# An adaLN transformer block on one core: q and k in two float32r parts and 64-row tiles instead of three bf16 parts and the full array

## The reference, cut to what matters

```python
h = layernorm(x) * (1 + ca) + sa
x = x + ga * attention(h)        # 16 heads of width 16, causal
h = layernorm(x) * (1 + cb) + sb
x = x + gb * ffn(h)              # layernorm, attention with 32 heads of width 8,
                                 # no mask, then 2 experts per batch with gelu
# in both attentions, for each head:
scores = q @ k.T / sqrt(d)       # 512 x 512, q and k are fp32
attn   = softmax(scores)
out    = attn @ v
```

## Time and profile before

| | |
|---|---|
| median of 3 runs | 1867.98 us (1866.65 to 1868.94) |
| profiled execution, first to last instruction | 1866.4 us |
| PE matmul busy | 1646.4 us, 88% |
| PE weight load busy | 717.9 us, 38% |
| VectorE busy | 1197.6 us, 64% |
| ScalarE busy | 1020.4 us, 55% |
| GpSimd busy | 479.6 us, 26% |
| moved by DMA | 152.61 MB |
| chain that ended last | PE 67%, DVE 9%, DMA 7% |

### The profile page before, as it was taken

One profiled execution on the slowest core, in us unless ns is written; L12 is line 12 of the kernel. 1 busy time (PEld: TensorE's weight loads), 2 busy tenths in 40 slices (PEclk: granted clock), 3 DMA queues, 4 the chain that ended last, 5 costly groups with the idle time before them and its releaser, 6 DMA issues.

```text
span 1866.4 us, 32448 instructions
## 1 busy us (share of the span) xinstructions
PE 1646.4 (88%) x8721; PEld 717.9 (38%) x8721; DVE 1197.6 (64%) x3093; ACT 1020.4 (55%) x1967; POOL 479.6 (26%) x804
## 2 busy tenths in 40 slices
PE   3487769999899989999899989999899997989887
PEld 1223313336333543346333443335333452325325
DVE  7466367864787567864787557964687566665440
ACT  0044425765567555765467645765467654665561
POOL 7133312232232222331232221331231232200100
PEclk9789869999999999999899999999999999999898
DMA  4540162243443452243334342243324243132301
GB/s 113 124 96 20 55 134 62 61 93 82 114 92 81 84 130 55 61 99 81 103 81 95 78 130 62 69 94 87 103 72 95 73 100 72 35 63 68 97 2 57
DMA packets 92282, 152.61 MB, mean 82 GB/s; under 512 B 19748, under 2 KB 78180, under 8 KB 83820
## 3 DMA queue, kind: packets, MB, share of 16 engines
q1 hardware_dynamic: 92100, 150.40, 33.8%
HBM read 119.58 MB, written 29.59 MB: 80 GB/s over the span
## 4 chain that ended last, share of the span: by engine, by line
PE 67%; DVE 9%; DMA 7%; issue 6%; ACT 6%; SPq 3%; POOL 1%; DVEq 0%; POOLq 0%; ACTq 0%
PE bank_out L1058 14%; PE bank_scores L1042 13%; PE bank_max L1021 12%; PE bank_side L993 6%; PE bank_side L1148 5%; DMA q_stack<-max_parts 4%; PE bank_side L1006 3%; PE bank_misc L1132 3%; DVE neg_max L1250 3%; PE bank_side L1132 3%; ACT probs L855 2%; PE bank_side L1113 2%; SPq L646 2%; PE bank_misc L1067 2%; PE bank_misc L1103 1%
## 5 line engine op out<-in xcount | busy, mean ns | idle before, releaser
L855 ACT ACTIVATE probs<-bank_scores 128x512 f32<-128x512 f32 (+3 forms) x1536 | 790.4, 544 | 629.8 <-PE bank_scores L1042 624.9
L1250 DVE TENSOR_REDUCE neg_max<-bank_max 128x1 f32<-128x512 f32 x1024 | 668.7, 682 | 266.1 <-PE bank_max L1021 261.7
L1042 PE MATMUL bank_scores<-q_stack,k_stack 128*128 128x512 bf16 (+3 forms) x1536 | 555.2, 366 | 70.0 <-DMA q_stack<-max_parts 42.6
L1021 PE MATMUL bank_max<-k_stack,q_stack 125*128 125x512 bf16 (+3 forms) x1536 | 559.2, 372 | 58.7 <-issue 21.5
L1058 PE MATMUL bank_out<-probs,v_tile 128*9 128x512 f32 (+4 forms) x3072 | 367.6, 551 | 1.0 <-POOL probs L766 0.9
L1247 DVE CUSTOM_DVE_ANT_0 bank_max<-bank_max,causal 128x128 f32<-128x128 f32 (+3 forms) x512 | 247.4, 506 | 183.7 <-PE bank_max L1021 180.0
L1021 PEld LDWEIGHTS bank_max<-k_stack,q_stack 125*128 125x128 bf16 x1536 | 150.1, 99 | 441.3 <-issue 293.8
L1042 PEld LDWEIGHTS bank_scores<-q_stack,k_stack 128*128 128x128 bf16 x1536 | 151.4, 99 | 309.5 <-ACT probs L855 153.2
L748 POOL CAST max_parts<-max_row 16x128 bf16<-16x128 f32 x96 | 26.8, 279 | 593.7 <-DVE max_row L1261 593.4
L766 POOL TENSOR_SCALAR_AFFINE_SELECT probs<-probs 128x512 f32<-128x512 f32 x128 | 81.1, 634 | 343.4 <-ACT probs L855 343.4
L1148 PE MATMUL bank_side<-w_out,hidden_T 128*128 128x256 f32 x512 | 132.6, 386 | 13.7 <-ACT hidden_T L891 10.7
(11 more groups left out here) (115 smaller groups left out, 1388.1 us busy)
## 6 DMA issues: line engine op xcount, KB each, us to landing
q_stack<-q_parts SPq DMA_DIRECT2D x96, 192.0 KB
w_in<-in_L_ffn_w_dram SPq DMA_DIRECT2D x16, 1024.0 KB, 5.9
w_out<-in_L_ffn_w_dram SPq DMA_DIRECT2D x16, 1024.0 KB, 9.4
q_parts<-partsq SPq DMA_DIRECT2D x32, 384.0 KB, 2.6
k_parts<-partsk SPq DMA_DIRECT2D x32, 384.0 KB, 2.5
k_stack<-k_parts SPq DMA_DIRECT2D x96, 128.0 KB, 6.5
k_stack<-k_parts SPq DMA_DIRECT2D x32, 256.0 KB, 7.5
q_stack<-q_parts SPq DMA_DIRECT2D x16, 384.0 KB, 4.6
```

The costliest lines, as they stand in the source:

```text
L855: nc.scalar.activation(probs[s % 2][:, k, q0:S], region[bank][:, q0:S], ACT.Exp, scale=float(WIDTH[a]) ** -0.5).then_inc(drained[bank], 1)
L1021: pe.matmul(region[bank][:, 0:keys], q_stack[buf][0:r, hh, qt * P:(qt + 1) * P], k_stack[buf][0:r, hh, 0:keys], start=True, stop=True).the ...
L1042: pe.matmul(region[bank][:, q0:S], k_stack[buf][:, h, kt * P:(kt + 1) * P], q_stack[buf][:, h, q0:S], start=True, stop=True).then_inc(fill ...
L1250: v.tensor_reduce(dst, region[bank], AX_X, ALU.max).then_inc(drained[bank], 1)
```

## The change

q and k are split into two float32r parts instead of three bf16 parts. Three pairs of 16 rows or four pairs of 8 rows (with 16 rows of zeros in the q stack) make 48 contraction rows, and the maxima become two rows: 48 rows for a maxima product, 50 for a score product. Each stack buffer holds four heads in rows 0 to 63 and four in rows 64 to 127. In a slot the maxima product takes a head of one half and the score product one of the other half (`tile_of`, `turned`). Pairs are laid out in DRAM already, so that a stack is four DMAs; a q or k tile is stored with two or three DMAs. GpSimd's part of `qk` is gone, and two of its four operations for the maxima. One `parts` buffer serves q and k: ScalarE's first k copy waits until q is stored. The lead of maxima is now counted in steps (one block of queries of four heads) and is 8; the maxima rows are made two steps after the last product. The constant rows of the stacks are filled by DMA at the start, from a tile of ones, and four blank regions of DRAM are written; PE waits for both. The weights' staging moves from the q stacks to `w_in` and `w_out`.

```diff
-LEAD = 7
+LEAD = 8
...
-Q_PARTS = ((0, 1, 2, 0, 1, 0), (0, 1, 2, 0, 1, 2, 0, 1, 2))
-K_PARTS = ((0, 0, 0, 1, 1, 2), (0, 1, 2, 1, 2, 0, 2, 0, 1))
-M_PARTS = 3
+Q_PARTS = ((0, 1, 0), (0, 1, 0, 1))
+K_PARTS = ((0, 0, 1), (0, 0, 1, 1))
+PARTS = 2
+TILES = 2
+TILE_ROWS = 64
+PRODUCT_ROWS = 48
...
 UNITS = ((0, 1), (2, 3, 4, 5))
-PRODUCT_ROWS = 96
-ZEROED_UNITS = (2, 3, 4)
+STACKS = 3
 T_STEPS = 4
 VALUES_SLOT = 3
+ROWS_AFTER = 2
 ROWS_SLOT = 1
 NORMALISE_SLOT = 2
 LN_PIECES = 5 + ROOT_STEPS
...
+def tile_of(k):
+
+    return k * TILES // GROUP
+
+
+def column_of(g, k):
+
+    per = GROUP // TILES
+    return g % (UNIT_HEADS // GROUP) * per + k % per
+
+
+def turned(k):
+
+    return (k + GROUP // 2) % GROUP
...
+STORED = [[2 * len(runs(order[a])) for order in (Q_PARTS, K_PARTS)] for a in range(2)]
...
-            waiting.setdefault((p + 1, ROWS_SLOT), []).append(("max_rows", lead[p][0], lead[p][1], lead[p][2] // GROUP))
+            waiting.setdefault((p + ROWS_AFTER, ROWS_SLOT), []).append(("max_rows", lead[p][0], lead[p][1], lead[p][2] // GROUP))
...
-    ahead = heads_of_attention(0, 0) + heads_of_attention(1, 0)
+    ahead = steps_of_attention(0, 0) + steps_of_attention(1, 0)
...
             def qk(b, turn, f, a, t, oc):
 
-                n = 2 * t + oc
-
-                wait_apart(sp, split_made[a], 4 * b + n + 1)
+                bank, _ = f[0]
+                wait_apart(sp, drained[bank], number(f[0], turn) + 1)
                 dram = (q_dram, k_dram)[t][a][b % 2]
                 dst = dram[:, oc * P:(oc + 1) * P, :] if a == 0 else dram[oc]
-                sp.dma_start(dst.rearrange("i p s -> p i s"), parts[t][:, :, oc, :]).then_inc(parts_stored[a], 16)
+                dst = dst.rearrange("i p s -> p i s")
+                src = parts[:, :, oc, :].bitcast(F32)
+                for g, part, n in runs((Q_PARTS, K_PARTS)[t][a]):
+                    sp.dma_start(dst[:, g:g + n, :], src[:, part:part + n, :]).then_inc(parts_stored[a], 16)
 
             def stacks(b, turn, f, u):
                 a = 0 if u in UNITS[0] else 1
                 d = WIDTH[a]
-                buf = buffer_of(u, b)
-                wait_apart(sp, parts_stored[a], 16 * 4 * (b + 1))
+                wait_apart(sp, parts_stored[a], 16 * sum(STORED[a]) * (b + 1))
                 wait_apart(sp, *buffer_free(u, b))
-                at = u % 2 * UNIT_HEADS * S
-                for dram, stack, order in ((q_dram, q_stack, Q_PARTS[a]), (k_dram, k_stack, K_PARTS[a])):
+                at = u % 2 * UNIT_HEADS
+                per = GROUP // TILES
+                for dram, stack, rows in ((q_dram, q_stacks, PRODUCT_ROWS), (k_dram, k_stacks, d * len(K_PARTS[a]))):
                     src = dram[0][b % 2] if a == 0 else dram[1][b % 2, (u - 2) // 2]
-                    src = src.rearrange("i (d h) s -> (i d) (h s)", d=d)[:, at:at + UNIT_HEADS * S]
-                    dst = stack[buf][:, :, :].rearrange("p h s -> p (h s)")
-                    for g, part, n in runs(order):
-                        sp.dma_start(dst[g * d:(g + n) * d, :], src[part * d:(part + n) * d, :])\
-                          .then_inc(stack_loaded[u], 16)
-                if u in ZEROED_UNITS:
-
-                    sp.dma_start(k_stack[buf][rows_of(1):PRODUCT_ROWS, :, :].rearrange("p h s -> p (h s)"), zero_dram[:, :])\
-                      .then_inc(stack_loaded[u], 16)
+                    src = src.rearrange("i (d h) s -> (i d) h s", d=d)[0:rows, at:at + UNIT_HEADS, :]
+                    src = src.rearrange("r (g t k) s -> t r g (k s)", t=TILES, k=per)
+                    for t in range(TILES):
+                        dst = stack[buffer_of(u, b)][t * TILE_ROWS:t * TILE_ROWS + rows, :, :].bitcast(F32)
+                        sp.dma_start(dst.rearrange("r (g k) s -> r g (k s)", k=per), src[t]).then_inc(stack_loaded[u], 16)
 
             def max_rows(b, turn, f, a, g):
                 groups = HEADS[a] // GROUP
                 u = unit_of(a, g * GROUP)
-                r, h = P - M_PARTS, g * GROUP % UNIT_HEADS
-                wait_apart(sp, max_split[a], 4 * groups * b + 4 * g + 4)
-                for m in range(M_PARTS):
-                    dst = q_stack[buffer_of(u, b)][r + m:r + m + 1, h:h + GROUP, :].rearrange("p h (q t) -> p (h q) t", t=P)
-                    sp.dma_start(dst, max_parts[:, g % 2, m, :]).then_inc(max_stored[a][g % 2], 16)
+                wait_apart(sp, max_split[a], 2 * groups * b + 2 * g + 2)
+                per = GROUP // TILES
+                at = column_of(g, 0)
+                for m in range(PARTS):
+                    dst = q_stacks[buffer_of(u, b)][PRODUCT_ROWS + m:P:TILE_ROWS, at:at + per, :].bitcast(F32)
+                    sp.dma_start(dst.rearrange("t k (q c) -> t (k q) c", c=P), max_parts[:, g % 2, m, :].bitcast(F32))\
+                      .then_inc(max_stored[a][g % 2], 16)
...
+            sp.wait_ge(ones_made, 1)
+            spared = PRODUCT_ROWS - WIDTH[0]
+            for n in range(STACKS):
+                for t in range(TILES):
+                    rows = k_stacks[n][t * TILE_ROWS + spared:(t + 1) * TILE_ROWS, :, :].bitcast(F32)
+                    sp.dma_start(rows, ones.broadcast_to([spare, UNIT_HEADS // TILES, S])).then_inc(ones_in, 16)
+            blank = len(Q_PARTS[1])
+            sp.wait_ge(ones_made, 2)
+            for n in range(2):
+                for oc in range(C):
+                    dst = q_dram[1][n, oc, blank:PRODUCT_ROWS // WIDTH[1]].rearrange("i p s -> p i s")
+                    sp.dma_start(dst, x_res[:, :, :].rearrange("p t d -> p (t d)").rearrange("p (i s) -> p i s", s=S))\
+                      .then_inc(ones_in, 16)
             sp.wait_ge(mod_rows_made, 6)
...
-                if t == 0 and oc == 0:
+                if oc == 0 and t == 0:
 
                     other, count = previous(a, b)
-                    wait(act, parts_stored[other], 64 * count)
-                nc.scalar.activation(parts[t][:, 0, oc, :], region[bank], ACT.Copy).then_inc(top_made[a], 1)
+                    wait(act, parts_stored[other], 16 * sum(STORED[other]) * count)
+                elif oc == 0:
+                    wait(act, parts_stored[a], 16 * sum(STORED[a]) * b + 16 * STORED[a][0])
+                nc.scalar.activation(parts[:, 0, oc, :], region[bank], ACT.Copy).then_inc(top_made[a], 1)
...
+            pe.wait_ge(ones_in, 16 * (TILES * STACKS + 2 * C))
...
-            def maxima(b, turn, f, a, h, qt):
-                u = unit_of(a, h)
-                buf, hh, r = buffer_of(u, b), h % UNIT_HEADS, P - M_PARTS
-                if hh == 0 and qt == 0:
-                    wait(pe, stack_loaded[u], 16 * stack_dmas[u] * (b + 1))
+            def maxima(b, turn, f, a, s, k):
+                g, qt = s // T, s % T
+                u = unit_of(a, g * GROUP)
+                if g * GROUP % UNIT_HEADS == 0 and qt == 0 and k == 0:
+                    wait(pe, stack_loaded[u], 16 * 2 * TILES * (b + 1))
                 bank, _ = f[0]
                 keys = (qt + 1) * P if CAUSAL[a] else S
                 start_fill(f[0], turn)
-                pe.matmul(region[bank][:, 0:keys], q_stack[buf][0:r, hh, qt * P:(qt + 1) * P],
-                          k_stack[buf][0:r, hh, 0:keys], start=True, stop=True).then_inc(filled[bank], 1)
-                maxima_fill[h // GROUP] = f[0]
+                kk = turned(k)
+                first, at = tile_of(kk) * TILE_ROWS, column_of(g, kk)
+                rows = slice(first, first + PRODUCT_ROWS)
+                pe.matmul(region[bank][:, 0:keys], q_stacks[buffer_of(u, b)][rows, at, qt * P:(qt + 1) * P],
+                          k_stacks[buffer_of(u, b)][rows, at, 0:keys], start=True, stop=True).then_inc(filled[bank], 1)
+                maxima_fill[g] = f[0]
...
-                h = (g * GROUP + k) % UNIT_HEADS
-                pe.matmul(region[bank][:, q0:S], k_stack[buf][:, h, kt * P:(kt + 1) * P], q_stack[buf][:, h, q0:S],
+                first, at = tile_of(k) * TILE_ROWS, column_of(g, k)
+                rows = slice(first, first + PRODUCT_ROWS + PARTS)
+                pe.matmul(region[bank][:, q0:S], k_stacks[buffer_of(u, b)][rows, at, kt * P:(kt + 1) * P], q_stacks[buffer_of(u, b)][rows, at, q0:S],
                           start=True, stop=True).then_inc(filled[bank], 1)
...
-                if n >= 2:
-                    wait(dve, split_made[a], 4 * b + n - 1)
-                else:
-                    other, count = previous(a, b)
-                    wait(dve, split_made[other], 4 * count)
-                v.tensor_tensor(rest[:, n % 2, :], region[bank], parts[t][:, 0, oc, :], ALU.subtract)\
+                v.tensor_tensor(parts[:, 1, oc, :], region[bank], parts[:, 0, oc, :].bitcast(F32), ALU.subtract)\
                     .then_inc(drained[bank], 1)
 
-            def maxima(b, turn, f, a, h, qt):
-                g = h // GROUP
+            def maxima(b, turn, f, a, s, k):
+                g, qt = s // T, s % T
                 bank, _ = f[0]
```

(3 more changed lines are left out.)

104 lines of the change are left out of this document (34 added, 70 removed).

## The result

| | before | after |
|---|---|---|
| median of the runs | 1868.4 us | 1967.8 us (1960.3 to 1984.1, 4 runs) |
| ratio, 95% interval | | 1.0545 (1.0499 to 1.0591) |
| profiled execution, first to last instruction | 1866.4 us | 1982.2 us |
| mean granted clock, median of the runs | 0.953 | 0.9175 |
| PE busy | 88% | 91% |

The change costs 5.4%, some 100 us. The forecast was 1910 us. The sign is right, the size is not: the miss is 58 us, and the time lies 3 us above the range. The profiled execution of the kernel after is the slowest of its runs; single steps are read from it, totals from the ratios.

A forecast was written before the change was run, and what follows sets the result against it. PE was taken as the bound in loaded steps, PE with two score banks in bare ones. Terms of -21.5 + 14.1 + 11.3 + 2.8 - 1 = +5.7 us a batch, x 8, + 2 gave 1910 us; range 1775 to 1965.

The forecast's parts named there:

- (a): Maxima and score products on PE: run together in different 64-row tiles at one column per cycle; 21.5 us a batch gained.
- (b): PE passages between 64-row products and 128-row side work: 153 new changes of tiling at 0.092 us, 14.1 us a batch lost.
- (c): Weight loads left uncovered on PE after changes of tiling, for side work and float32r products: 11.3 us a batch lost.
- (e): Single parts buffer: ACT's first k copy waits for the q store, PE with it; 2.8 us a batch lost.
- (d): Precision split of q/k and maxima: POOL operations go, ACT's copy and DVE's subtraction stay; nothing gained directly.
- (f): Maxima rows ahead of the score: fewer POOL operations and DMA issues, four stack DMAs instead of nine; 1 us a batch gained.
- (g): Program start: PE waits for DMA loads of ones and stores of blanks; 2 us lost once.
- first rival: Changes between 128 and 64 rows on PE drain nothing, loads stay covered; faster, 1796 us, chance 0.33.
- Rivals 2 and 3: On PE, float32r takes two cycles a column (2100 us, chance 0.11); tiles run one after the other (2035 us, chance 0.07).
- Rival 4: ACT's wait for the q store is 3 us and more, as stores compete with stack loads; 1960 us, no chance given.

The follow-up runs named there:

- `bf16_tiles`: Changed kernel with bf16 in place of float32r for parts, stacks, maxima rows and DRAM copies; same tiles, pairs and order: 1834.0 us, 0.9804 of the kernel before.
- `rows_66`: Changed kernel with bf16, all score and maxima products contracting rows 0 to 65 on the full array, no attention: 1865.4 us, 0.9990 of the kernel before.
- `bf16_full`: Changed kernel with bf16 and products over 112 and 114 rows, without tiles or pairs, no attention: 1803.8 us, 0.9656 of the kernel before.
- `rows_64`: Changed kernel with bf16, all score and maxima products contracting rows 0 to 63, one tile, never paired, no attention: 2012.7 us, 1.0772 of the kernel before.
- `parts_apart`: Changed kernel with separate q and k parts buffers again and without ScalarE's wait for the q store: 1972.3 us, 1.0524 of the kernel before.
- `two_parts`: Kernel before with q, k and maxima in two bf16 parts instead of three; full array, layout, start and lead kept: 1801.0 us, 0.9644 of the kernel before.
- `bf16_same_tile`: Changed kernel with bf16, maxima product taken from the same 64-row tile as its score, so nothing pairs: 2022.2 us, 1.0832 of the kernel before.
- `same_tile`: Changed kernel, float32r kept, maxima product taken from the same 64-row tile as its score, so nothing pairs: 2265.0 us, 1.2116 of the kernel before.

## Why the prediction was wrong in size

Two numbers price the clock. At a mean clock c, a span has 2 x (1 - c) of its time at the lower level: 176 us before, 325 us after, by the medians of the runs. And a microsecond there costs about 0.4 us: runs of one kernel differ so (`bf16_tiles` 1830.2 us at 0.936 and 1850.5 at 0.921, 58 us more at the lower level and 20 us longer, 0.35; the kernel after 0.43 by its fastest and slowest run), and `rows_66` against `bf16_full` gives 62 us for 168, 0.37. With that taken out of each difference of ratios, the whole change splits so (us for the program; the intervals of the ratios alone leave some 10 us on each). The measured column is made of differences from one kernel to the next, so that its sum has to be the whole; that it fits proves none of its lines:

| term | forecast | measured | from |
|---|---|---|---|
| (a) pairs | -172 | -124 | `bf16_tiles` less `bf16_full`, less the line below and 49 of clock |
| (b), and side loads of (c) | +154 | +103 | `rows_64` less `rows_66`, 146, less 43 of clock |
| (c) loads of the products | +49 | +107 | after less `bf16_tiles`, 138, less 31 of clock |
| (e) parts buffer | +22 | within the noise | `parts_apart` |
| (d), (f), (g) | -6 | -44 | `bf16_full` less before, -64, less -20 of clock |
| granted clock | 0 | +60 | 149 us more at the lower level |
| sum | +47 | +102 | 1.0545: +102 |

The forecast's own sum was 47 us above 1868, 1915 us, written down as 1910; and half of 0.105 at 121 entries is 6.35 us a batch, not 6.1, which is 2 us in all. Neither matters here.

**(a) and (b)** belong together: pairs and changes with their side loads were to give -18 us and gave -21. In a loaded step the prices hold one by one: 4 x 0.22 less for the pairs, 4 x 0.09 for changes and 2 x 0.105 for side loads is -0.31, and 4.54 became 4.27 with bf16. Both are smaller in the whole than their counts say: 1144 changes (counted; the forecast had 153 x 8 = 1224) at 0.093 are 106 us and with the side loads near 150, where 103 were measured; the pairs gave 124, not 172. A part of either lies in steps where banks or DVE bind. How much of each, no run tells apart. The Trainium skill (TensorEngine Tiling (Array Packing), Key Properties) has the rule that a change of tiling mode drains TensorE. The runs agree: product to side work takes 0.31 us with 64 rows and 0.21 with 66, and the two kernels differ by 146 us. With it the first rival falls, which had 1796 us.

**(c) is the step that failed**, with the clock below. "each meets a float32r load of unknown length, 0 to 0.105 us; at the middle 6.1 us": it is the upper end, 0.105, on every entry into the products. With 121 entries a loop turn and 1144 / 153 = 7.5 turns' worth, that is 95 us of the 107; a load that waits for a bank pays as well, and a product whose load is covered still takes some 0.017 us more than with bf16 (second pair to the values 0.326 us and 0.309), which no term had. (The doubled transfers are in the 107 too: PE's two rows for stacks and maxima rows sum to 15.8 us after, to 5.9 in `bf16_tiles`.) The other part of (c), the loads of side work, was right, and stands in the line of (b): a q piece's first matmul takes 0.533 us to the next instead of 0.428, an identity transpose's 0.166 instead of 0.109, about the half that was taken. The row to go by was in the forecast: f32 weights load in 0.19 us, and float32r is as wide. The Trainium skill (TensorE: Matmul & The Clock Gate, Weight-path perf modes — Fast Weight Load (FWL) and DoubleRow) says that the fast load is not on for an FP32 input; the load records, 183 to 202 ns for float32r against 94 to 99 for bf16, agree if float32r counts as such.

**The clock** had no term, and the forecast gave no reason to leave it out; it is as large as the miss of (c). That "after the start the clock stands at its upper level" was carried over from the kernel before to one with narrower products. The runs showed 0.9175 for 0.953, 149 us more at the lower level, some 60 us.

**(e)** sized the landing (4.0 and 4.8 us for 3.4 to 3.7 and 4.2 and more) and ACT's wait nearly right: 21.8 us in 15 waits, 2.7 a batch where the mark was 2.5. What failed is that PE would stand with ACT: without the wait the time is the same within the noise.

**(f)** took 1 us a batch off a wait that is 42.6 us in the waits view, and looked only inside the loop, where it is short. With (g) the gain is 38 us larger than forecast. **(g)** seems to have had the wrong sign: the second batch's input is issued at 35.4 us after the start instead of 42.6, and the first maxima product starts at 74.8 instead of 81.8. No run has the start apart.

Rivals 2 and 3 fall with the starts of the pairs. Rival 4 named 1960 us, near the time measured, by a wait whose cost is too small to tell: the number alone would have confirmed the wrong cause. The miss of 58 us is made of (c), 58 too low, and the clock, 60, of which (f) with (g), and (e), took 60 back; (a) and (b) with its side loads miss by 48 and 51, one against the other.

## What to carry to other kernels

Before packing products into smaller tiles, price three things: each passage between the two tilings (0.09 us here), the weight load that a passage or a bank wait uncovers (0.105 us for a 4-byte type, nothing visible for bf16), and what narrower products do to the granted clock. Try the cheap half of a change alone: here two bf16 parts on the full array (`two_parts`, 1801 us) take all of the gain and none of the three prices, with less precision than either kernel. And when a wait is to be removed, read its total in the waits view and where in the program its parts stand; a turn of the loop times the number of batches leaves out the start and the end.

## What was not expected of the hardware

- **The granted clock falls with the rows that products contract.** Same instructions but for the row count, same full array: 112 rows 0.965, 66 rows 0.921 (medians of the runs). In 64-row products that never pair it is 0.900 (`rows_64`) and 0.889 (`bf16_same_tile`), with float32r 0.8365 (`same_tile`, 741 us at the lower level). The clock falls after the same 4.5 us gap of PE in both of the first two; what differs is how long PE then works at 1.2 GHz. What the rows hold seems not to matter: in `two_parts` the maxima products contract 126 rows, most of the q stack's being zeros, at 0.971. Why is not shown.
- **float32r** streams nearly as fast as bf16 (512 columns with a covered load: the next product after 0.237 us on the full array, 0.220 with bf16) but loads weights like f32 (records of 183 to 202 ns, 94 to 99 for bf16). Its price over bf16, with twice the bytes to store and load, was 97 us on the full array.
- **Two 64-row products in different tiles** start within 10 ns and take one product's time (the next bf16 pair after 0.22 to 0.23 us), and a change between 64 and 128 rows costs as much as one to 32-column strips (0.09 us, product to side work and score to values both 0.31).
- Whether the start's lower clock (5s to 7s in the first sixth of the kernel after) has the same cause as that at the loop's edges was not tried.
